# Recurrent layer of a four-layer kernel: the meeting of the engines moved ahead of the group norm, and the end of a batch's layer moved into the next batch

## The reference, cut to what matters

```python
sx = concat([state[i0+1], xa[:, :-1]]) - xa              # xa = _ln(x)
t = tanh((xa + sx * maa_x) @ maa_w1)                      # small matrices that mix the five inputs
...                                                       # xw, xk, xv, xr, xg; w, k, v, r; g = silu(xg @ Wg.T)
_, outs = scan(step, s0, (k, v, w, r))                    # s = k v + w s, out = r (faaaa k v + s)
y = group norm of outs over each head                     # mean, variance, root
x = x + (y * gn_w + gn_b) * g @ Wo.T                      # gate and projection
xc = _ln(x)                                               # second norm
sxc = concat([state[i0], xc[:, :-1]]) - xc
rr = sigmoid((xc + sxc * fmaa_r) @ fWr.T)                 # feed-forward part
kk = square(relu((xc + sxc * fmaa_k) @ fWk.T))
x = x + rr * (kk @ fWv.T)
```

## Time and profile before

| | |
|---|---|
| median of 3 runs | 1328.41 us (1323.9 to 1329.78) |
| profiled execution, its own time | 1327.49 us |
| its span | 1325.7 us |
| recurrent layer, four batches | 197.2 to 477 us of the span |
| TensorE busy | 1231.7 us (93%) |
| VectorE busy | 805.6 us (61%) |
| ScalarE busy | 536.6 us (40%) |
| GpSimd busy | 180.3 us (14%) |

### The profile page before, as it was taken

How to read it: one execution, slowest core, us unless ns; L and a number is a source line. 1 busy time by engine, 2 the same in 40 slices (tenths; PEclk the granted TensorE clock), 3 DMA queues, 4 the chain that set the end, 5 groups by cost and what they waited for, 6 DMA issues and landing times.

```text
span 1325.7 us, 17907 instructions
## 1 busy us (share of the span) xinstructions
PE 1231.7 (93%) x6056; PEld 865.4 (65%) x6064; DVE 805.6 (61%) x2386; ACT 536.6 (40%) x1233; POOL 180.3 (14%) x397
## 2 busy tenths in 40 slices
PE   7687988898989788999999899999999999999999
PEld 4365655464645343444443588888888888888877
DVE  4443337686868346777785566666656666666520
ACT  3144353343534323545455343433343434443432
POOL 3022014021212121102011100000000000000000
PEclk9688699998999889999999999999999999999999
DMA  7433633101111544534424913030303030500000
GB/s 226 141 101 112 204 115 123 72 32 64 40 56 48 153 144 153 181 117 133 164 73 144 318 63 128 1 128 0 128 0 128 0 128 0 191 0 1 1 9 24
DMA packets 100651, 127.59 MB, mean 96 GB/s; under 512 B 6736, under 2 KB 78576, under 8 KB 98320
## 3 DMA queue, kind: packets, MB, share of 16 engines
q1 hardware_dynamic: 99936, 126.14, 29.2%
q10 hardware_dynamic: 624, 0.30, 0.1%
HBM read 79.33 MB, written 46.79 MB: 95 GB/s over the span
## 4 chain that ended last, share of the span: by engine, by line
PE 80%; DMA 7%; DVE 5%; ACT 3%; issue 2%; POOL 2%; SPq 1%; ACTq 0%; POOLq 0%; DVEq 0%
PE TT L2453 8%; PE J L2445 8%; PE J L2465 8%; PE TT L2429 4%; PE S L2419 4%; PE OO L1079 4%; PE OO L2419 4%; PE OO L1076 4%; PE J L324 2%; PE S L636 2%; PE J L1079 2%; PE J L1345 2%; PE OO L2686 2%; DMA km<-query_parts 2%; PE J L1076 2%
## 5 line engine op out<-in xcount | busy, mean ns | idle before, releaser
L2523 ACT ACTIVATE PT<-TT 128x512 f32<-128x512 f32 x128 | 76.4, 597 | 282.8 <-PE TT L2429 282.8
L2604 DVE TENSOR_SCALAR QK<-J,cols 128x256 f32<-128x256 f32 x126 | 61.0, 484 | 70.0 <-PE J L2445 70.0
L2558 POOL COPY On<-probs 128x8 f32<-128x8 f32 x128 | 29.2, 228 | 471.3 <-DVE probs L2593 442.1
L2593 DVE TENSOR_SCALAR probs<-probs,inv 128x257 f32<-128x257 f32 x256 | 79.1, 352 | 4.5
L1079 PE MATMUL OO<-ctxT,weights_a 128*128 128x512 f32 x136 | 69.7, 637 | 12.0 <-SPq L308 9.4
L2429 PE MATMUL TT<-ident,probs 128*128 128x128 f32 x512 | 76.9, 273 | 2.6 <-DVE probs L2593 2.6
L1076 PE MATMUL OO<-weights_a,ctxT 128*128 128x512 f32 x136 | 68.9, 631 | 9.8 <-SPq L308 6.1
L2429 PEld LDWEIGHTS TT<-ident,probs 128*128 128x128 f32 x512 | 63.9, 141 | 16.3 <-DVE probs L2593 3.4
L2599 DVE COPY km<-TT 128x256 f32<-128x256 f32 x128 | 54.2, 423 | 30.8 <-PE TT L2453 30.5
L2453 PE MATMUL TT<-PT,weights_a 128*128 128x256 f32 x256 | 66.6, 383 | 0.0
L2465 PE MATMUL J<-early,km 128*128 128x256 f32 x256 | 65.8, 379 | 0.3 <-DVE km L2599 0.3
(11 more groups left out here) (414 smaller groups left out, 2706.2 us busy)
## 6 DMA issues: line engine op xcount, KB each, us to landing
wide_keys<-weights_a SPq DMA_DIRECT2D x64, 256.0 KB, 2.1
wide_values<-weights_a SPq DMA_DIRECT2D x56, 256.0 KB, 2.0
query_parts<-weights_a SPq DMA_DIRECT2D x48, 192.0 KB, 2.8
weights_a<-wide_keys SPq DMA_DIRECT2D x16, 512.0 KB, 7.2
weights_a<-wide_values SPq DMA_DIRECT2D x16, 512.0 KB, 8.2
early<-wide_keys SPq DMA_DIRECT2D x16, 512.0 KB, 8.1
early<-wide_values SPq DMA_DIRECT2D x16, 512.0 KB, 8.7
weights_a<-key_parts SPq DMA_DIRECT2D x16, 288.0 KB
```

The lines of the kernel that those rows point to most:

```text
L2523: act.activation(PT[:, n % 2, :], T0[:, :], ACT.Copy).then_inc(pt3_ready, 1)
L2593: ins = dve.tensor_scalar(P_[n % 2][:, qt, :], P_[n % 2][:, qt, :], inv[:, qt, n % 32:n % 32 + 1], None, ALU.mult)
L2604: dve.tensor_scalar(QK[:, n % 2, 0, 0:S], J0[:, 0:S], head_cols(f"bq{a + 1}")[:, h:h + 1], float(DIM3) ** -0.5, ALU.add, ALU.mult).then_in ...
```

## The change

The meeting is placed between the sums into `yv` and the group norm. The group norm (`group_moments`), its root (`take_group_root`) and scale and gate (`group_scale`) of batch b now stand in the opening of batch b + 1: the moments behind `xxx`, the root ahead of the two Tanh on ScalarE, the scale ahead of the mixes. `flip_out` and `project_out` come behind the mix matmuls, `add_out` and `normalise_xc` later among the mixes. `flip_xc` stands in step 1 of the scan (in bank S1), `fetch_xc` ahead of step 3 of ScalarE's loop, `mix_channels` in step 2 of VectorE's loop, and the feed-forward's projections in steps 3, 4 and 5. In every batch `turn_y(1, O1)` stands one unit earlier, and the centring of the next batch's input (`front_dve_last`) stands behind the first mix. Batch 3 keeps its own end.

```diff
@@ TensorE, opening @@
                     project_ahead(pe, O1, u0)
-                    if b_before is not None:
-                        flip_out()
                     pe.wait_ge(xxx_ready, 1)
...
                     mm.then_inc(lora_done, 1)
-                    if b_before is not None:
-                        project_out(1)
                     pe.wait_ge(lora_ready, 1)
...
+                    if b_before is not None:
+                        flip_out(1)
                     pe.wait_ge(xv_ready, 1)
                     project(pe, J1, lambda k, o: w["L1_v"][:, k, o * P:(o + 1) * P], xf[2], KC, vT_done)
                     if b_before is not None:
-                        flip_xc(1)
+                        project_out(1)
...
+                    if b_before is not None:
+                        pe.wait_ge(x_ready, 1)
                     spread(0)
@@ TensorE, scan and end @@
                         if b_before is not None:
-                            if j == 0:
+                            if j == 1:
+                                pe.wait_ge(v_ready, 1)
+                                flip_xc(1)
+                            if j == 3:
                                 project_fk(1)
-                            if j == 2:
+                            if j == 4:
                                 project_fr(1)
-                            if j == 4:
+                            if j == 5:
                                 project_fv(1)
...
+                    turn_y(1, O1)
                     pe.wait_ge(bonus_ready, 1)
                     pe.wait_ge(hT_ready, 1)
                     ahead_late(0)
-                    turn_y(1, O1)
@@ ScalarE @@
+                    def take_group_root(turn):
+                        act.wait_ge(gvar_ready, turn)
+                        act.activation(root, var, ACT.Sqrt).then_inc(groot_ready, 1)
+
                     copy_ahead(act, O1, u0)
                     if b_before is not None:
-                        fetch_out(1)
+                        take_group_root(1)
                     act.wait_ge(lora_done, 1)
                     act.activation(lora, J0[:, 0:S], ACT.Tanh)
                     act.activation(lora_last, J0[0:DMIX, S:2 * S], ACT.Tanh).then_inc(lora_ready, 1)
+                    if b_before is not None:
+                        fetch_out(1)
...
-                    if b_before is not None:
-                        fetch_xc(b_before, 1)
...
                     copy_ahead(act, J0, u0 + 1)
+                    if b_before is not None:
+                        fetch_xc(b_before, 1)
                     for j in range(3, DIM1):
...
-                            if j == 3:
+                            if j == 5:
                                 square_relu(1)
-                            if j == 4:
                                 sigmoid_r(1)
-                            if j == 6:
+                            if j == 7:
                                 fetch_fv(1)
...
-                    act.wait_ge(gvar_ready, 1)
-                    act.activation(root, var, ACT.Sqrt).then_inc(groot_ready, 1)
+                    if following == 2:
+                        take_group_root(2)
@@ VectorE @@
                     ins.then_inc(xxx_ready, 1)
+                    if b_before is not None:
+                        group_moments()
                     front_dve_first(following, dve, chain, b_next)
-                    front_dve_last(following, dve, b_next)
                     if b_before is not None:
-                        add_out(b_before, 1)
+                        group_scale(1)
...
                     mix(0, ORDER[0])
+                    front_dve_last(following, dve, b_next)
                     mix(1, ORDER[1])
-                    if b_before is not None:
-                        normalise_xc(b_before, 1)
...
                     mix(3, ORDER[3])
+                    if b_before is not None:
+                        add_out(b_before, 1)
...
                     mix(4, ORDER[4])
                     if b_before is not None:
-                        mix_channels(1)
+                        normalise_xc(b_before, 1)
...
                         dve.tensor_tensor(read[j % 4], rT, state[j % 2][:, :, 0:S], ALU.mult).then_inc(read_ready, 1)
+                        if j == 2 and b_before is not None:
+                            mix_channels(1)
...
+                    if following == 2:
+                        group_moments()
+                        group_scale(2)
@@ GpSimd @@
-                    if b_before is not None:
-                        root_of_tail(1)
                     for n, f in enumerate(ORDER[1:4]):
...
+                    if b_before is not None:
+                        root_of_tail(1)
```

More of the change, by code:

```diff
@@ L1820, in pe_program, with flip_out @@
                 pe.wait_ge(loaded["ahead"], 16)
-                def flip_out():
+                def flip_out(turn):
+                    pe.wait_ge(yg_ready, turn)
                     flip(pe, T0, yv.rearrange("p (t c) -> p t c", t=TQ), yg_flipped)
@@ L1830, in flip_xc @@
                     pe.wait_ge(xc_normed, turn)
[L1831 removed]
+                    flip(pe, xc_bank(turn), xc, xc_flipped)
                 def project_fk(turn):
@@ L1988, in main @@
                         ahead_late(1)
-                        pe.wait_ge(yg_ready, 1)
-                        flip_out()
+                        flip_out(1 if b_before is None else 2)
                         ahead_late(2)
```

47 lines of the change are left out of this document (26 added, 21 removed).

## The result

The changed kernel takes 1344.67 us (median of 4 runs, 1340.51 to 1347.25) against 1327.33 us of the kernel before (4 runs, 1323.9 to 1329.78): ratio 1.0127, 95% interval 1.0096 to 1.0158. It is slower, by 1.3%. Run again later, it gave 1.0138 (1.0096 to 1.0180). Two executions of all those in this document, one of gaps_filled_idly (7129.81 us) and one of parts_two_stores_later (3256.61 us), were slow ones and are left out of the ratios.

A forecast was written before the change was run, and what follows sets the result against it. TensorE, busy 93% of the span, was taken as the bound. Terms of -9.9, -5.6, -0.4, +9.9, +9.9 and +8.0 sum to +11.9 on 1327.49 us, giving 1339.5 us, range 1326 to 1348.

The forecast's parts named there:

- The meeting: TensorE's idle time between batches, three times: 1.4 us instead of 4.7, so -9.9 us in all.
- Rival 4: SyncE comes late with its stores, so the meeting isn't earlier: +27 us, 1355 us; chance 0.05.
- The clock behind the meeting: TensorE's work behind the three meetings: the clock holds at full after the shorter gap, -5.6 us.
- Batch 0: The first mix no longer stands behind the centring, so TensorE's wait of 0.41 us goes: -0.4 us.
- The wait for the Tanh: TensorE ahead of the mixes in three openings: a new gap of 3.3 us each, +9.9 us in all.
- rival 5: ScalarE's table switches cost more than their load: +3.8 us over three openings, 1343.3 us; chance 0.04.
- The wait for the fourth read: TensorE ahead of `gather(1)` in three scans: new gaps of 3.3 us (3.05 if GpSimd's slowing falls elsewhere), +9.9 us.
- The half clock in the new gaps: TensorE behind the six new gaps: the clock falls in five, at 1.6 us each, +8.0 us.
- The end of batch 3 unchanged.: Batch 3 from its last `gather` on: no change, since the root there waits behind other work of ScalarE.
- VectorE's scale is off the path, by 0.5 us.: In the openings, the group's scale and first mix end about 0.5 us before they would delay TensorE.

The follow-up runs named there:

- gaps_filled_idly: The changed kernel with throwaway matmuls on TensorE in the six new gaps, ahead of the mixes and of `gather(1)`: 1332.06 us, ratio 1.0036 to the kernel before.
- parts_two_stores_later: Changed kernel with root and mix_channels later, real units and throwaway matmuls filling gaps; SyncE's next-layer key and query transfers two unit stores later in batch 3: ratio 0.9924.
- before_filled_at_meeting: The kernel before with eight throwaway matmuls ahead of each of the three meetings inside the layer: 1317.45 us, ratio 0.9934.
- root_behind_tanh: The changed kernel with ScalarE's root of the group norm behind the two Tanh instead of ahead: 1341.56 us, ratio 1.0122 to the kernel before.
- mix_channels_later: The changed kernel with `mix_channels` behind the fourth read and `project_fk` one step later: 1330.38 us, ratio 1.0034 to the kernel before.
- before_turn_y_early: The kernel before with only `turn_y(1, O1)` one unit earlier and `front_dve_last` behind the first mix: 1316.12 us, ratio 0.9932.
- root_and_mix_late: The changed kernel with the root behind the Tanh and `mix_channels` behind the fourth read: 1325.71 us, ratio 0.9991 to the kernel before.

## Why the prediction was right, point by point

**The meeting** (-9.9). Measured 1.48, 1.47 and 1.60 us, in place of 4.7: -9.6. Taken at 1.4. From the end of ScalarE's last copy (314.41) to TensorE's start (315.24) it is 0.83 us; 0.45 + 0.35 = 0.80 was taken for the release and the store. Rival 4 (SyncE late) didn't occur.

**The clock behind the meeting** (-5.6). At 1.00 behind all three. Confirmed, and by itself in before_filled_at_meeting.

**Batch 0** (-0.4). The 0.41 us ahead of v is gone.

**The wait for the Tanh** (+9.9). Measured 3.12, three times: +9.4. The chain (variance, root, load, Tanh) is as it was written. The chance that lay in rival 5 can be checked on the rows shown above: the Tanh starts 0.02 us behind its load (320.26 + 1.28 = 321.54, then 321.56), and TensorE's gap is 3.12 us. The drain of about 1.38 us that the Trainium skill gives in "ScalarE: Activation LUTs", "What ACT_TABLE_LOAD costs", would have made it about 4.5 (3.12 + 1.38, an estimate); the trace doesn't agree, and the measurement decides.

**The wait for the fourth read** (+9.9). Measured 3.89, 3.80 and 3.79: +11.5, above the stated upper value of 3.7. The term was mis-sized, by one operation. `mix_channels` takes longer where it now stands, beside GpSimd's work; VectorE and GpSimd of the changed kernel, scan of batch 3:

```profile
420.54 1.56 DVE L2241 TENSOR_TENSOR weights_a<-weights_a 128x512 f32<-128x512 f32 x1
422.13 1.67 DVE L2246 SCALAR_TENSOR_TENSOR weights_a<-weights_a,cols 128x256 f32<-128x256 f32 x4
...
420.13 1.42 POOL L2207 TENSOR_TENSOR probs<-V,QK 128x512 f32<-128x512 f32 x1 [1.24 <-ACT QK L2120]
```

Its first operation took 0.68 us in the opening, and 1.56 here. I had named this stretch, but only as something that falls away from the read, for the 3.05. It did fall away from the read (-0.65), and fell on `mix_channels` (+0.88), which the read waits for just as well: 3.7 - 0.65 + 0.88 = 3.9, the gap measured. The row agrees with the page "SBUF — State Buffer" of the Trainium skill, section "SBUF: two separate sides", by which the engine that comes second waits for the whole operation of the first: GpSimd ends at 421.55, 1.01 us behind VectorE's start, and 1.01 + 0.68 would be 1.69, near the 1.56 measured.

**The half clock in the new gaps** (+8.0). Five of six fell, as taken; they cost 9.6 us, since one, in the third opening, lasted 6.9 us instead of 3.6. Repeated, six of six fell. gaps_filled_idly shows the term by itself: 8.2 us of the layer, 9.7 without batch 0. "This decides" was right: +3.9 without it would have been no measurable change.

**"The end of batch 3 unchanged."** Wrong. The kernel before, at the rows that answer 460.18 and 475.69 of the changed kernel:

```profile
445.85 1.11 PE L316 MATMUL TT<-ident,probs 128*128 128x128 f32 x4 [6.15 <-DVE probs L2348]
460.54 5.42 PE L1079 MATMUL S<-ctxT,weights_a 128*128 128x512 f32 x12 [1.56 <-ACT weights_a L1092]
```

From `flip_out` to the next layer it is 33.5 us (460.18 to 493.66) against 31.0 (445.85 to 476.82): +2.5. The wait behind the transfers is 2.78 us instead of 1.56, and behind it the clock fell, 1.7 us. Why the transfers took 17.7 us here and 16.9 before, with the same instructions, isn't settled; the wait was between 1.56 and 4.86 us over the kernels of this study.

**"VectorE's scale is off the path, by 0.5 us."** Right for the change, and close: when the Tanh no longer held the mixes back (root_behind_tanh), it came on the path at once.

The sum with what was measured: -9.6 - 5.6 - 0.4 + 9.4 + 11.5 + 9.6 + 2.5 = +17.4 us, by the profile's layer +19.2. The 1.8 us between are spread over the batches and not traced to a row. The medians differ by 17.3 us. The prediction had +11.9: its signs and its mechanism held, and 1.6 us at the fourth read, 1.6 at the clock and 2.5 at the end of batch 3 were missing. These three misses all have the same sign, and the forecast of 1339.5 us was 5.2 too low, and the periods of batches 1 and 2 came out at 66.9 and 68.8 us, the second above the 68 forecast.

Two slips of its arithmetic don't change this. 1327.49 + 11.9 is 1339.4. And six falls of the clock at 2.3 us each end at 1345, not at the 1348 given as the upper end (2.7 each would give it); the measured 1344.67 lies just under either.

## What to carry to other kernels

When a wait is moved, the fill that used to cover other waits moves with it. List what each engine's queue loses ahead of every wait that it still has, and put the fill there in the same step: the early meeting was 1.3% slower without it, and 0.8% faster with it and with two operations put later. Then ask what the move itself was worth: one line of the order and throwaway matmuls gave the kernel before the same 0.9%, without the move. Price a gap of TensorE as its length and the half clock behind it. Before reordering anything for such a gap, fill it with throwaway matmuls: eight of them at each meeting of the kernel before were worth 0.7%, for two lines. And follow a tail to the chain that bounds it: a held clock won only 0.7 us there.

## What the runs showed of the hardware

- Gaps of 3.1 to 3.9 us were followed by a granted clock of 0.5 to 0.6 in 11 of 12 cases (the changed kernel, two executions), for stretches of 3.5 to 6.9 us; with mix_channels_later and root_behind_tanh it is 16 of 18. Gaps of 1.3 to 1.7 us at the meetings behind batches 0 to 2 and at `gather(1)` left it at 1.00. Between them the length doesn't decide: in batch 3's end the clock fell behind 2.17 us (before_filled_at_meeting, 0.57) and held behind 2.79 (before_turn_y_early, 1.00). And in root_behind_tanh the clock fell behind waits of 0.73, 0.56 and 0.86 us that followed each other, in one opening of three, and likewise in root_and_mix_late; in gaps_filled_idly it was at 0.50 behind the 1.39 us ahead of batch 0, where waits of 0.81, 0.81 and 0.47 us had gone before. So the single gap isn't all that counts.
- The throwaway matmuls held the clock at 1.00 in every gap that they filled.
- A VectorE operation on two inputs took 1.56 us instead of 0.68 where a GpSimd operation ran beside it, in all three scans.
- A store of 256 KB took 8.0 to 9.2 us, to the copy that waited for it, in the 14 profiles, where it stood behind the key and query parts, 576 KB twice among them, against a median of 2.1 us over all such stores.
